# Attention: the reciprocals of the heads' sums as one power of minus one on GpSimd, in place of two reciprocals on VectorE

## The chip, the core and the metric

The kernel runs on one core of one Trainium2 chip. The metric is the device time of one execution in microseconds (us); the figure compared is the median over runs. The engines go by short names in the profile: PE is TensorE, DVE is VectorE, ACT is ScalarE, POOL is GpSimd, and SP is the engine whose queue issues nearly all of this kernel's DMAs. Each engine runs its own instruction stream in order, and semaphores tie the streams together.

## What is computed

The reference is one layer of a hybrid network on an input of 4 x 1024 tokens with 256 channels: attention with 16 heads of 16 channels, a feed-forward layer with ternary weights, a memory layer with a scan over time, and the feed-forward layer again, each behind a layer norm and with a residual. The change lies in the attention, which is cut to this:

```python
def _L0_attn_a_ref(x, ln_gamma, ln_beta, w_qkv, b_qkv, w_out, b_out):
    h = (x - mu) * rsqrt(var + 1e-05) * ln_gamma + ln_beta
    qkv = (h @ w_qkv + b_qkv).reshape(B, T, 3, NUM_HEADS, HEAD_DIM)
    scores = einsum('bhqd,bhkd->bhqk', q, k) / sqrt(HEAD_DIM)
    attn = softmax(scores, axis=-1)
    out = einsum('bhqk,bhkd->bhqd', attn, v)
    return x + out.reshape(B, T, C) @ w_out + b_out
```

## The kernel before

The kernel has three stages on a time axis: `project` (queries, keys and values, to about 105 us), `attend` (to about 795 us) and `mix_and_remember` (the rest). The change is in `attend`.

`attend` works through NG = 16 groups of four heads; four groups make one batch. Each group has two halves of 512 queries (qc = 0, 1), and each half has eight blocks of 128 keys (kt). For each block PE makes four score matrices of 128 keys x 512 queries (`score`, L758), ACT takes their exponential into `prob` (L663), and PE multiplies `prob` by the values (`weigh`, L770) into `ps_o`. The values tile `v_ones` has 16 columns of values and 16 of ones for each head, so `ps_o` holds the unnormalised output and, beside it, the sum of the exponentials. At the end of each half ACT copies `ps_o` to `o_sb` (`take_o`, L653) and SP stores it in DRAM as `oT` (`store`, L577).

The softmax needs each query's maximum before its scores are made. PE therefore computes the scores a second time, one half-group to one group ahead, for the maxima only (`score_for_max`, L747), into two buffers of `ps_m`. DVE reduces them (`maxima`, L684, 16 reductions of 128 x 1024 for each half). PE may not write a buffer of `ps_m` before DVE has reduced what it holds, and PE issues this work in between the scores and the weighing of the current half (`scores_ahead`). After the 16 reductions DVE makes five small steps: L687 takes the maximum of two interleaved parts of the tile `maxes`, which lies in SBUF, so both of its inputs are in SBUF; L689 and L691 negate and split; L696 transposes. SP then writes the transposed rows to DRAM (`place_max`, L569) and, when they have landed, reads them back into two rows of the queries' stack (L573). PE's first score of the half waits for this (`m_in`).

The division by the sums is done later, by reciprocals. For the three early batches (groups 0 to 11) the sums are gathered in one DMA into the tile `sums`, 96 partitions x 512 (L612, issued at the start of group 13). DVE inverts them in place in two operations of 96 x 256 (`invert`, L706), one behind each half of `maxima` of group 14, which DVE runs while PE is still in group 13 and early in group 14. SP, in its turn for group 14, first places the maxima of the half, then waits for both halves of `inverted` (L588), stores the reciprocals in DRAM (L589), waits for that store, issues eight loads for the first two chunks of the next stage (`load_heads`, L508 and L510), and only then stores group 14's first output and places the maxima of group 15's first half. POOL multiplies the loaded heads by the loaded reciprocals (`divide_heads`, L516). All these DMAs go through SP's one queue.

POOL has little to do in `attend`: it copies the values of a group into `v_ones` when the slot is free (`place_v`, L622); behind the copy for group 15, its last, come two small products (L636, L637) and then the wait of `divide_heads` for chunk 0. In other stages POOL computes powers: `scalar(const, which, shape)` gives one column of the tile `scalars`, repeated over the shape without a copy, and `tensor_tensor(..., ALU.pow)` raises a tile to that power. L101 and L245 do this with -0.5 on tiles of 2 to 8 columns.

Of the kernel before, what the change touches and what calls it, by code (L numbers as in the profile page):

```python
# [11 lines left out]
ALU = mybir.AluOpType  # L12
# [6 lines left out]
B, T, C = 4, 1024, 256  # L19
TOK = B * T  # L20
H, HD = 16, 16
CH = C // P
CHUNK = 512
# [3 lines left out]
LN_EPS = 1e-5  # L27
RMS_EPS = 1e-6
# [54 lines left out]

SCALARS = (-0.5, LN_EPS, RMS_EPS, 1.0, 0.0)
S_MINUS_HALF, S_LN_EPS, S_RMS_EPS, S_ONE, S_ZERO = range(5)


def scalar(const, which, shape):  # L90
    col = const["scalars"][:, which:which + 1]
    for _ in shape[2:]:
        col = col.unsqueeze(len(col.shape))
    return col.to_broadcast(shape)
# [10 lines left out]
NG = B * H // GH  # L105
# [28 lines left out]
def load_stacks(sp, qk_parts, stacks, g, slot):  # L134

    for qk, stack, part in ((0, stacks["q"], Q_PART), (1, stacks["k"], K_PART)):
        src = qk_parts[qk, bass.ds(g * CG, CG)].rearrange("(hp par d) a t -> par d a hp t", par=2, d=HD)
        for par, base in enumerate(BASES):
            for i in range(PAIRS):
                sp.dma_start(stack[slot][base + i * HD:base + (i + 1) * HD], src[par][:, part[i]]).then_inc(stacks["loaded"][slot], 16)  # L140


def project(nc, cols, rows, const, w, qk_parts, stacks, v_all, x_all, heads, rows_1):
# [5 lines left out]
    with ExitStack() as ctx:  # L149
# [73 lines left out]
        def _(pool):  # L223
# [3 lines left out]
            for tile, value in ((ident[:], 0.0), (ones[:], 1.0), (ln_mul[:, 0:1], 1.0), (ln_mul[:, 1:2], 1.0 + LN_EPS),  # L227
                                (ln_add[:, 0:1], LN_EPS), (ln_add[:, 1:2], LN_EPS ** 2)):
                made.did(pool.memset(tile, value))
            for j, value in enumerate(SCALARS):  # L230
                made.did(pool.memset(const["scalars"][:, j:j + 1], value))
# [260 lines left out]
def sums_of(oT, batches, per_head):  # L492

    rows = slice(batches.start * NG // B * P, batches.stop * NG // B * P)
    return oT[rows].rearrange("(h r) (j t) -> r h j t", r=2 * HD, j=per_head)[HD]


def inverses_of(inverse, batches, per_head):
    return inverse[batches.start * H:batches.stop * H].rearrange("h (j t) -> h j t", j=per_head)


def load_heads(sp, oT, inverse, heads, n):
    b, half = divmod(n, T // CHUNK)
    at = slice(half * CHUNK, (half + 1) * CHUNK)
    for c in range(CH):
        rows = (NG // B * b + 2 * c) * P
        src = oT[rows:rows + 2 * P, at].rearrange("(h two d) t -> two h d t", two=2, d=HD)[0]
        sp.dma_start(heads["o"][n % 2][:, c], src).then_inc(heads["loaded"][n % 2], 16)  # L508
        sums = inverse[H * b + H // CH * c:H * b + H // CH * (c + 1), at]
        sp.dma_start(heads["inverse"][n % 2][:, c], sums.unsqueeze(1).to_broadcast([H // CH, HD, CHUNK])).then_inc(heads["loaded"][n % 2], 16)  # L510
# [8 lines left out]
def attend(nc, rows, const, x_all, qk_parts, stacks, v_all, oT, inverse, heads, rows_1):  # L519
# [4 lines left out]
    with ExitStack() as ctx:  # L524
        def sb(name, shape, dt=F32):
            return ctx.enter_context(nc.sbuf_tensor(name, shape, dt))

        def sem(name):
            return ctx.enter_context(nc.semaphore("p2_" + name))
# [29 lines left out]
        sums, per_head = sb("sums", [2 * H * (B - 1), CHUNK]), 2  # L559
        sums_in, inverted, inverse_out = sem("sums_loaded"), sem("inverted"), sem("inverses_stored")  # L560
# [3 lines left out]
        @block.sync  # L564
        def _(sp):
            def place_max(g, slot, qc):
                half = QC * g + qc
                sp.wait_ge(m_turned, half + 1)
                sp.dma_start(neg_rows[qc].rearrange("(a b) (c i) -> c (a b) i", a=2, c=4), negT[qc][:]).then_inc(m_stored[qc], 16)  # L569
                sp.wait_ge(m_stored[qc], 16 * g + 16)  # L570
                rows_of = neg_rows[qc].rearrange("(a hp par t) q -> par a hp (t q)", a=2, hp=HP, par=2)
                for par, base in enumerate(BASES):
                    sp.dma_start(q_st[slot][base + MROW:base + ROWS, :, qc * CHUNK:(qc + 1) * CHUNK], rows_of[par]).then_inc(m_in[qc], 16)  # L573

            def store(g, qc):
                sp.wait_ge(o_taken, QC * g + qc + 1)
                sp.dma_start(oT[bass.ds(g * P, P), qc * CHUNK:(qc + 1) * CHUNK], o_sb[qc][:]).then_inc(o_out[qc], 16)  # L577

            def group(g, u, load_ahead=True, first=False, last=False, inverses=False):
                if load_ahead:  # L580
                    if not first:
                        sp.wait_ge(exp_done, EXPS * g + S_RING)
                    load_stacks(sp, qk_parts, stacks, g + 2, (u + 2) % SLOTS)
                if not first:
                    store(g - 1, 1)
                place_max(g, u, 1)
                if inverses:
                    sp.wait_ge(inverted, 2)  # L588
                    sp.dma_start(inverses_of(inverse, early, per_head), sums[:]).then_inc(inverse_out, 16)  # L589
                    sp.wait_ge(inverse_out, 16)  # L590
                    load_heads(sp, oT, inverse, heads, 0)
                    load_heads(sp, oT, inverse, heads, 1)
                if not last:
                    store(g, 0)
                    place_max(g + 1, (u + 1) % SLOTS, 0)
                else:
                    sp.wait_ge(out_ready, 2)
                    load_heads(sp, oT, inverse, heads, 2)
                    store(g, 0)
                    store(g, 1)  # L600

            place_max(0, 0, 0)
            for g in range(3):
                group(g, g, first=g == 0)
            for it in range(1, 4):
                for u in range(3):
                    group(3 * it + u, u)
            for g in range(12, NG):
                if g == NG - 3:
                    sp.wait_ge(o_out[0], 16 * g)  # L610
                    sp.wait_ge(o_out[1], 16 * (g - 1))
                    sp.dma_start(sums[:], sums_of(oT, early, per_head)).then_inc(sums_in, 16)  # L612
                group(g, g % 3, load_ahead=g + 2 < NG, last=g == NG - 1, inverses=g == NG - 2)
            for s in o_out:
                sp.wait_ge(s, 16 * NG)

        @block.gpsimd
        def _(pool):
            def place_v(g, slot, first=False):
                if not first:  # L620
                    pool.wait_ge(pv_done, UNITS * (g - 2) + 2)
                pool.tensor_copy(v_st[slot][:, :, :, 0:HD],  # L622
                                 v_all[:, bass.ds(g, 1)].rearrange("p g k (h d) -> p (g k) h d", d=HD)).then_inc(v_set, 1)

            for i in range(SLOTS):
                pool.memset(v_st[i][:, :, :, HD:], 1.0).then_inc(ones_set, 1)
                place_v(i, i, first=True)
            for n in range(NCH):
                at = x_all[:, TPC * n:TPC * n + TPC]
                pool.tensor_tensor(at, at, rows[:, ROW_BOUT:ROW_BOUT + 1].to_broadcast([P, TPC, C]), ALU.add).then_inc(bias_added, 1)  # L630
            for it in range(1, 5):
                for u in range(3):
                    place_v(3 * it + u, u)
            place_v(NG - 1, 0)
            norm_g = rows[:, ROW_NORMG:ROW_NORMG + 1]
            pool.tensor_tensor(const["w_gate"][:], const["w_gate"][:], norm_g.to_broadcast([P, CH, C]), ALU.mult).then_inc(bias_added, 1)  # L636
            pool.tensor_tensor(rows[:, ROW_GB:ROW_GB + 1], rows[:, ROW_GB:ROW_GB + 1], norm_g, ALU.mult).then_inc(bias_added, 1)  # L637
            divide_heads(pool, heads, 0)
            divide_heads(pool, heads, 1)
            pool.wait_ge(var_ready, 1)  # L640
            inverse_deviation(pool, Steps(pool, dev_steps), rows_1["mv"][:, 0, 0, :, 1], const, rows_1["tmp"][:, 0, 0], rows_1["rstd"][:, 0, 0], rstd_ready)
            divide_heads(pool, heads, 2)
            pool.wait_ge(bias_added, NCH + 2)
            pool.wait_ge(heads["divided"], 2)
# [32 lines left out]
        def _(dve):  # L677
# [22 lines left out]
            for g in range(2):  # L700
                maxima(g + 1, 0)
                maxima(g + 1, 1)
            def invert(k):
                dve.wait_ge(sums_in, 16)
                at = slice(k * CHUNK // 2, (k + 1) * CHUNK // 2)
                dve.reciprocal(sums[:, at], sums[:, at]).then_inc(inverted, 1)  # L706

            for it in range(1, 5):
                for u in range(3):
                    for qc in range(QC):  # L710
                        maxima(3 * it + u, qc)
                        if 3 * it + u == NG - 2:
                            invert(qc)
            maxima(NG - 1, 0)
            maxima(NG - 1, 1)

# [1525 lines left out]
```

## Time and profile before

| | us |
|---|---|
| median of 2 runs (lowest, highest) | 1155.38 (1152.81, 1157.96) |
| the profiled execution | 1156.36 |
| its span | 1154.3 |
| granted clock of PE, mean of the profiled execution | 0.962 of full speed |
| PE busy | 1064.9 (92%) |
| DVE busy | 1002.0 (87%) |
| ACT busy | 808.4 (70%) |
| POOL busy | 244.3 (21%) |

The profiled execution is 1.0 us above the median, and 2.1 us of it lie outside its span. The busy shares are averages over three stages with different limits. The groups of instructions show what carries `attend`: 1024 exponentials of ACT (555.8 us), 512 reductions of DVE (606.7 us), and the three kinds of matmul of PE at L747, L758 and L770 (219.4, 260.5 and 327.9 us). POOL's copies at L622 have 530.1 us of idle time ahead of them.

### The profile page before, as it was taken

The page shows a single profiled execution, that of the slowest core. Times are in us where ns is not written, and L with a number is a line of the kernel's source. Part 1 is how long each engine was busy: PE and PEld are TensorE (multiplying, and loading weights), DVE is VectorE, ACT ScalarE, POOL GpSimd, SP SyncE. Part 2 cuts the span into 40 slices and gives each one's busy share as a digit, 9 for nine tenths or more (in the row PEclk, how much of TensorE's full clock was granted, in tenths as well). Part 3 has the DMA queues.
Part 4 walks back from the last instruction along what each step waited for, and adds up shares of the span by engine and source line. Part 5 has one row for each costly group of instructions (what it writes and reads, how often), then busy time and mean ns, then how long its engine had stood idle before and what let it go on. Part 6 is the DMA issues. An engine that isn't in the chain of part 4 may idle for free. (4 is left out here: it accounts for less than half of the span.)

```text
span 1154.3 us, 22163 instructions
## 1 busy us (share of the span) xinstructions
PE 1064.9 (92%) x8566; PEld 582.3 (50%) x8566; DVE 1002.0 (87%) x1469; ACT 808.4 (70%) x1654; POOL 244.3 (21%) x345
## 2 busy tenths in 40 slices
PE   5997799999999999999999998997899998799995
PEld 4885233333333333333333333334667766688984
DVE  7776999999999999999999999943499998569887
ACT  4452288888888888888888887873568687343443
POOL 6423300000000000000000000102254333665643
PEclk9898599999999999999999999998899998899997
DMA  8595304414422440442244040211134325634321
GB/s 271 152 316 192 56 13 75 67 25 63 67 48 41 75 65 24 65 67 48 41 75 67 26 68 20 84 53 38 63 111 141 116 79 162 195 85 134 102 74 55
DMA packets 87332, 101.55 MB, mean 88 GB/s; under 512 B 21884, under 2 KB 57212, under 8 KB 87228
## 3 DMA queue, kind: packets, MB, share of 16 engines
q1 hardware_dynamic: 86396, 98.56, 35.8%
q8 instruction: 67, 1.10, 0.4%
q10 hardware_dynamic: 832, 1.58, 0.4%
q14 instruction: 37, 0.30, 0.1%
HBM read 55.09 MB, written 43.88 MB: 86 GB/s over the span
## 5 line engine op out<-in xcount | busy, mean ns | idle before, releaser
L663 ACT ACTIVATE prob<-ps_s 128x512 f32<-128x512 f32 x1024 | 555.8, 597 | 124.5 <-PE ps_s L758 107.6
L684 DVE TENSOR_REDUCE maxes<-ps_m 128x2 f32<-128x1024 f32 x512 | 606.7, 1217 | 18.1 <-PE ps_m L747 14.7
L770 PE MATMUL ps_o<-prob,v_ones 128*32 128x256 f32 x4096 | 327.9, 392 | 7.7 <-issue 7.3
L758 PE MATMUL ps_s<-q_stack,k_stack 64*128 64x512 f32 x1024 | 260.5, 499 | 0.0
L747 PE MATMUL ps_m<-k_stack,q_stack 62*128 62x512 f32 x1024 | 219.4, 422 | 17.9 <-DVE maxes L684 14.2
L758 PEld LDWEIGHTS ps_s<-q_stack,k_stack 64*128 64x128 f32 x1024 | 99.0, 184 | 211.3 <-ACT prob L663 187.6
L770 PEld LDWEIGHTS ps_o<-prob,v_ones 128*32 128x32 f32 x4096 | 81.7, 108 | 192.1 <-issue 102.7
L622 POOL COPY v_ones<-v_all 128x512 f32<-128x512 f32 x16 | 9.8, 614 | 530.1 <-PE ps_o L770 530.1
L747 PEld LDWEIGHTS ps_m<-k_stack,q_stack 62*128 62x128 f32 x1024 | 101.1, 192 | 35.2 <-DVE maxes L684 27.8
L405 ACT ACTIVATE p_parts<-ps_qk,cols 128x512 fp32r<-128x512 f32 x32 | 22.0, 687 | 39.2 <-PE ps_qk L450 33.2
L1385 PE MATMUL p_p<-p_hT,w_p 128*128 128x512 f32 x96 | 44.4, 613 | 2.6 <-ACT p_hT L1150 2.6
L516 POOL TENSOR_TENSOR heads<-heads,inverse 128x1024 f32<-128x1024 f32 x8 | 18.9, 2363 | 94.0 <-DMA inverse<-inverse_sums 94.0
L324 DVE SCALAR_TENSOR_TENSOR p_parts<-ps_qk,cols,p_parts 128x512 fp32r<-128x512 f32 x32 | 23.7, 745 | 11.9 <-ACT p_parts L405 11.5
L1313 PE MATMUL p_a<-w_gate,p_hT 128*128 128x256 f32 x128 | 31.5, 400 | 0.0
L1385 PEld LDWEIGHTS p_p<-p_hT,w_p 128*128 128x128 f32 x96 | 18.6, 197 | 23.5 <-issue 20.1
L99 POOL TENSOR_TENSOR ln_tmp<-ln_mv,scalars 128x4 f32<-128x4 f32 x16 | 11.1, 692 | 83.7 <-DVE ln_mv L73 83.7
L1313 PE MATMUL p_a<-w_out,heads 128*128 128x256 f32 x112 | 28.1, 408 | 0.1
L1313 PEld LDWEIGHTS p_a<-w_gate,p_hT 128*128 128x128 f32 x128 | 24.7, 198 | 4.3 <-issue 0.2
L69 DVE BATCH_NORM_STATS2 p_stats<-x_all 128x6 f32<-128x256 f32 x60 | 21.0, 413 | 6.1 <-DMA x_all<-in_x_dram 5.9
L1313 PEld LDWEIGHTS p_a<-w_out,heads 128*128 128x128 f32 x112 | 22.9, 210 | 3.8 <-issue 0.3
L1070 ACT ACTIVATE p_pre_kv<-p_p 128x512 f32<-128x512 f32 x8 | 4.8, 597 | 27.7 <-PE p_p L1385 27.7
L69 DVE BATCH_NORM_STATS2 ln_stats<-x_all 128x6 f32<-128x256 f32 x64 | 22.5, 414 | 0.6
(301 smaller groups left out, 1534.7 us busy)
## 6 DMA issues: line engine op xcount, KB each, us to landing
qk_parts<-p_parts SPq DMA_DIRECT2D x32, 512.0 KB, 7.4
q_stack<-qk_parts SPq DMA_DIRECT2D x96, 128.0 KB, 4.7
k_stack<-qk_parts SPq DMA_DIRECT2D x96, 128.0 KB, 7.7
oT<-o_sb SPq DMA_DIRECT2D x32, 256.0 KB, 4.1
x_all<-in_x_dram SPq DMA_DIRECT2D x8, 512.0 KB, 9.9
heads<-oT SPq DMA_DIRECT2D x16, 256.0 KB
inverse<-inverse_sums SPq DMA_DIRECT2D x16, 256.0 KB
out_dram<-x_all SPq DMA_DIRECT2D x7, 512.0 KB, 3.7
```

What stands on the lines that cost most here:

```text
L69: steps.did(dve.bn_stats(stats[:, i, :], src[:, i, :]))
L99: steps.did(pool.tensor_tensor(tmp, var, scalar(const, S_LN_EPS, tmp.shape), ALU.add))
L324: dve.scalar_tensor_tensor(out=r32(parts[:, n % 2, j, 1]), in0=ps_qk[:, j], scalar=cols[:, COL_BQK + j:COL_BQK + j + 1], in1=parts[:, n % ...
L405: act.activation(r32(parts[:, n % 2, j, 0]), ps_qk[:, j], ACT.Identity, bias=cols[:, COL_BQK + j:COL_BQK + j + 1]).then_inc(hi_ready, 1)
L516: pool.tensor_tensor(o[:], o[:], heads["inverse"][n % 2][:], ALU.mult).then_inc(heads["divided"], 1)
L663: act.activation(prob[at % P_RING][:, h], ps_s[:, (GH * at + h) % S_RING], ACT.Exp, scale=HD ** -0.5).then_inc(exp_done, 1)
L684: dve.tensor_reduce(maxes[:, i // 2, i % 2], ps_m[:, i % M_PAIRS], AX.X, ALU.max).then_inc(m_taken, 1)
L747: ins = pe.matmul(ps_m[:, i // 2 % M_PAIRS, i % 2], r32(q_st[slot][base:base + MROW, hp, q0:q0 + P]), r32(k_st[slot][base:base + MROW, hp, ...
L758: pe.matmul(ps_s[:, (GH * (UNITS * slot + KT * qc + kt) + h) % S_RING], r32(k_st[slot][rows, pair, kt * P:(kt + 1) * P]), r32(q_st[slot][r ...
L770: ins = pe.matmul(ps_o[32 * h:32 * h + 32, queries], v_st[slot][:, kt, h], prob[(UNITS * slot + KT * qc + kt) % P_RING][:, h, queries], st ...
L1313: ins = pe.matmul(ps_a[:, i // 2, i % 2], src[:, c, i * P:(i + 1) * P], weights[:, c], start=c == 0, stop=c == CH - 1)
L1385: ins = pe.matmul(ps_p[:, j], w_p[:, c, j * P:(j + 1) * P], hT[n % 2][:, c], start=c == 0, stop=c == CH - 1)
```

## The change

The list of constants gets a sixth entry, -1.0. `scalar` takes as many partitions as the shape asks for. The two reciprocals on DVE go. On POOL, behind the copy of values for group 15 and ahead of the two small products, comes a wait for the sums and one `tensor_tensor` with `ALU.pow` over the whole tile of 96 x 512, in place. SP waits for one step of `inverted` instead of two.

```diff
-SCALARS = (-0.5, LN_EPS, RMS_EPS, 1.0, 0.0)
-S_MINUS_HALF, S_LN_EPS, S_RMS_EPS, S_ONE, S_ZERO = range(5)
+SCALARS = (-0.5, LN_EPS, RMS_EPS, 1.0, 0.0, -1.0)
+S_MINUS_HALF, S_LN_EPS, S_RMS_EPS, S_ONE, S_ZERO, S_MINUS_ONE = range(6)
@@ scalar
-    col = const["scalars"][:, which:which + 1]
+    col = const["scalars"][0:shape[0], which:which + 1]
@@ attend, block.sync
                 if inverses:
-                    sp.wait_ge(inverted, 2)
+                    sp.wait_ge(inverted, 1)
@@ attend, block.gpsimd
             place_v(NG - 1, 0)
+            pool.wait_ge(sums_in, 16)
+            pool.tensor_tensor(sums[:], sums[:], scalar(const, S_MINUS_ONE, [2 * H * (B - 1), CHUNK]), ALU.pow).then_inc(inverted, 1)
@@ attend, block.vector
-            def invert(k):
-                dve.wait_ge(sums_in, 16)
-                at = slice(k * CHUNK // 2, (k + 1) * CHUNK // 2)
-                dve.reciprocal(sums[:, at], sums[:, at]).then_inc(inverted, 1)
-
             for it in range(1, 5):
                 for u in range(3):
                     for qc in range(QC):
                         maxima(3 * it + u, qc)
-                        if 3 * it + u == NG - 2:
-                            invert(qc)
```

## Rows read from the trace of the kernel before

**Rows 1.** The page's head: the span, and each engine's busy us and share.
```profile
span 1154.3 us, 22163 instructions
PE 1064.9 (92%) x8566; PEld 582.3 (50%) x8566; DVE 1002.0 (87%) x1469; ACT 808.4 (70%) x1654; POOL 244.3 (21%) x345
```
**Rows 2.** Windows (start:end, length, each engine's busy us, PE clock, DMA): half-groups without and with a reciprocal.
```profile
664.40:684.60 20.20, 19.97 (x194) 7.45 (x192) 19.64 (x21) 17.75 (x35) 2.40 (x3) 1.00 0.58 80
706.40:729.00 22.60, 20.94 (x188) 7.52 (x190) 20.88 (x22) 17.08 (x33) 0.00 (x0) 0.92 0.22 68
```
**Rows 3.** Waits, 664 to 750 us: PE for DVE's reductions (us in total, times, longest).
```profile
PE ps_m L747 <- DVE maxes L684: 3.2, 3, 1.4
```
**Rows 4.** Timeline of DVE (start, us, engine, line): L687 of one half; the two reciprocals.
```profile
672.62 0.19 DVE L687 TENSOR_TENSOR maxm<-maxes 128x16 f32<-128x16 f32 x1
...
693.60 1.71 DVE L706 RECIPROCAL sums<-sums 96x256 f32<-96x256 f32 x1
...
715.42 1.71 DVE L706 RECIPROCAL sums<-sums 96x256 f32<-96x256 f32 x1
```
**Rows 5.** Timeline of ACT: the copies that end halves, and group 15's first exponentials.
```profile
664.34 0.60 ACT L653 ACTIVATE o_sb<-ps_o 128x512 f32<-128x512 f32 x1
684.55 0.60 ACT L653 ACTIVATE o_sb<-ps_o 128x512 f32<-128x512 f32 x1
706.37 0.60 ACT L653 ACTIVATE o_sb<-ps_o 128x512 f32<-128x512 f32 x1
729.64 0.60 ACT L653 ACTIVATE o_sb<-ps_o 128x512 f32<-128x512 f32 x1
...
748.24 2.26 ACT L663 ACTIVATE prob<-ps_s 128x512 f32<-128x512 f32 x4 [0.22 <-PE ps_s L758]
```
**Rows 6.** All instructions of lines 245 and 101, powers on POOL (ns min/median/max).
```profile
L245 POOL TENSOR_TENSOR p_rstd<-p_var_eps,scalars x8: 1642/1703/1962, 7.4 to 67.6; 128x8 f32<-128x8 f32 x8
...
L101 POOL TENSOR_TENSOR ln_rstd<-ln_tmp,scalars x16: 1006/1009/1392, 773.9 to 950.9; 128x4 f32<-128x4 f32 x16
...
L101 POOL TENSOR_TENSOR p_rstd_last<-p_tmp_last,scalars x2: 696/696/697, 1140.3 to 1141.4; 128x2 f32<-128x2 f32 x2
```
**Rows 7.** Timelines of POOL and DVE: L687 started during POOL's sums and products, twice.
```profile
108.23 18.50 POOL L630 TENSOR_TENSOR x_all<-x_all,rows 128x1024 f32<-128x1024 f32 x8
...
124.41 2.37 DVE L687 TENSOR_TENSOR maxm<-maxes 128x16 f32<-128x16 f32 x1
...
736.20 2.37 POOL L516 TENSOR_TENSOR heads<-heads,inverse 128x1024 f32<-128x1024 f32 x1 [3.31 <-DMA inverse<-inverse_sums]
...
737.91 0.72 DVE L687 TENSOR_TENSOR maxm<-maxes 128x16 f32<-128x16 f32 x1
```
**Rows 8.** Timelines of POOL and DVE: a two-input DVE operation during a power of 8 columns.
```profile
10.49 1.68 POOL L245 TENSOR_TENSOR p_rstd<-p_var_eps,scalars 128x8 f32<-128x8 f32 x1
...
11.31 1.01 DVE L302 SCALAR_TENSOR_TENSOR p_wq_lo<-v_all,cols,p_wq_hi 128x768 fp32r<-128x768 f32 x1
...
12.25 1.05 POOL L247 TENSOR_TENSOR p_gain<-p_rstd,scalars 128x4 f32<-128x4 f32 x1
```
**Rows 9.** Timelines of SP and POOL: the sums, the reciprocals' store, group 15's maxima.
```profile
656.61 0.61 SPq L612 DMA_DIRECT2D sums<-oT  x1
...
664.25 0.62 POOL L622 COPY v_ones<-v_all 128x512 f32<-128x512 f32 x1 [39.79 <-PE ps_o L770]
...
718.75 0.39 SPq L589 DMA_DIRECT2D inverse_sums<-sums  x1
...
739.31 0.55 SPq L569 DMA_DIRECT2D neg_rows<-neg_maxT  x1
741.31 1.29 SPq L573 DMA_DIRECT2D q_stack<-neg_rows  x2
```
**Rows 10.** Windows as in Rows 2: PE behind the second reciprocal, and early in attention.
```profile
720.00:722.00 2.00, 2.00 (x14) 0.70 (x12) 1.60 (x2) 1.02 (x2) 0.00 (x0) 0.50 0.17 55
...
138.00:139.00 1.00, 1.00 (x11) 0.20 (x8) 1.00 (x2) 0.92 (x2) 0.00 (x0) 0.50 1.11 143
139.00:140.00 1.00, 1.00 (x12) 0.30 (x4) 0.86 (x1) 0.12 (x1) 0.00 (x0) 0.91 1.05 135
```

## The prediction, made before the changed kernel ran

> **What bounds the kernel now.** I read the page first: DVE is busy for 87% of the span and PE for 92%, POOL for 21% [rows 1]. Work that leaves DVE for POOL looks free by these shares, but they are averages, so I went to the windows of single half-groups around the change. A half without a reciprocal lasts 20.20 us, of which DVE is busy 19.64 and PE 19.97 [rows 2]. The two are locked together through the buffers of `ps_m`, and whatever delays DVE delays everything. The copies that end the halves show it: 20.21 us between the first two, 21.82 with the first reciprocal, 23.27 with the second [rows 5]. The waits name the cause, PE on DVE's reductions, once 1.4 us long behind each reciprocal [rows 3]. In the half with the second reciprocal PE's granted clock also falls, to 0.92 on average [rows 2] and to 0.50, its lower level of 1.2 GHz, from 720 to 722 us [rows 10]; PE had stood idle for the reduction just before.
>
> **What is removed.** Two reciprocals of 1.71 us [rows 4]. The first lengthened its half by 21.82 - 20.20 = 1.62 us. The second lengthened its own by 23.27 - 20.20 = 3.07 us, of which 1.45 is the slow clock. Together 4.7 us of the path. I take all of it, if no other wait takes their place.
>
> **What is added, by itself.** One power over 512 columns. The trace has powers of 2, 4 and 8 columns; their shortest durations are 696, 1006 and 1642 ns [rows 6]. The steps are (1006 - 696) / 2 = 155 and (1642 - 1006) / 4 = 159 ns a column, so the cost is 378 + 157 x columns, a straight line. Partitions lie side by side, so 96 instead of 128 save nothing that I count on. For 512 columns: 0.378 + 512 x 0.157 = 80.8 us, with 79.7 and 81.8 by the two slopes. From below, POOL's sum over 1024 columns takes 18.50 / 8 = 2.31 us [rows 7], so 1.2 us for 512, if the long tile ran at the rate of a plain operation. I take 80.8, because it comes from the same operation on the same engine and three sizes agree; the far end stays as a rival.
>
> It starts when POOL has copied the last values, at 664.25 + 0.62 = 664.87 us; the sums were asked for at 656.61 [rows 9], 8 us earlier, and are there. It ends at 664.9 + 80.8 = 745.7.
>
> **Where it lies: beside DVE.** POOL is idle at this time, and the power would be hidden if it touched nothing of DVE's. It does. L687 normally takes 0.19 us [rows 4]. Begun at 124.41, while POOL's sums ran until 108.23 + 18.50 = 126.73, it took 2.37 us and ended at 126.78. Begun at 737.91, while a product of POOL's ran until 738.57, it took 0.72 and ended at 738.63 [rows 7]. Both times it ended 0.05 us behind POOL: it did not slow down, it stood still until POOL's instruction was over. A power stands in the same place for far longer. L687 is due at 672.62, 7.8 us into the power. If it is held to the end, it ends at 745.7 + 0.05 instead of 672.81: 72.9 us later. L689, L691, the transpose and all later reductions are queued behind it on DVE; PE fills the two buffers of `ps_m` and stops within two steps; ACT runs out of scores. Nothing covers this.
>
> Against it stands one observation. A DVE operation with two SBUF inputs, L302, began at 11.31, inside a power of 8 columns that ran from 10.49 to 12.17, and took 1.01 us, ending at 12.32; it wasn't held. Right after it the order was turned round: POOL's L247, begun at 12.25, needed 1.05 us [rows 8] and waited for the next DVE operation. So a short power lets DVE in after at most 0.8 us, before its end. My reading is that POOL keeps DVE out while its inputs are still being read; 8 columns are read at the start, and the columns of a 512-column power are read as they are used, to within a few of the end. If the read-ahead is 8 columns, DVE is let in 8 x 0.157 = 1.3 us sooner. If instead the power reads in pieces with gaps, DVE gets in almost at once. The trace has no long power, so both ends stay: 72.9 and about 0. I take 72.9, since the two L687 cases are the same DVE instruction as here and the counter-example is 64 times shorter than the new operation.
>
> The Trainium skill says the same more sharply: "SBUF — State Buffer", section "Who interferes with whom", has GpSimd and a VectorE operation with two SBUF inputs exclude each other for the whole instruction, and whichever issues second blocks fully. The L687 rows agree with it; the 8-column power doesn't for its whole length. By this rule the sum is the one I take; by the counter-example it is that of the first rival.
>
> **The smaller terms.** POOL's L636 and L637 now follow the power and meet the DVE steps behind L687; where they alternate, L689 and L691 wait for them. Between 0 and 2 us; I take 1.0. PE has stood still for 70 us and starts at the lower clock: from 138 to 139 us it works with full busy time at 0.50, and is back at 0.91 in the next microsecond [rows 10]. The second reciprocal's episode cost 1.45 us. Between 0 and 4; I take 1.7. On SP the wait for the power is over long before its turn comes, since PE, ACT and DVE all stand still meanwhile: nothing. The extra constant is one more tiny fill at the start: nothing.
>
> **The sum**, against the profiled execution of 1156.4: 1156.4 + 72.9 + 1.0 + 1.7 - 4.7 = 1227.3. Against the median of the runs, which is 1.0 lower, it would be 1226.3. Nothing in the later stages can take this back, as they start only when attention ends. I give 1227.
>
> **Rival A: DVE is let in, and SP's queue becomes the bound.** The power still ends at 745.7, but DVE goes on. Without the reciprocals group 15's first exponentials are due at 748.24 - 4.7 = 743.5 [rows 5]. SP sits in its wait for `inverted` with the head loads, group 14's first store and group 15's maxima queued behind it. Before, the store of the reciprocals began at 718.75 [rows 9] and the last of the head loads had landed at 736.20, where POOL's product begins [rows 7]: 17.5 us. Now that is 745.7 + 17.5 = 763.2, and the maxima travel in the same queue behind them. After it come the read-back's two issues, 1.3 us [rows 9], and some 2 us of landing: 766.5. The first exponentials are 18.3 us later than before; with 1.7 for the clock the time is 1156.4 + 20.0 = 1176. If the small transfers pass the large ones, the maxima are issued after 7.5 us of head-load issues at 753.2, and with the 2.0 us from L569 to L573 [rows 9], 1.3 and 2 they land at 758.5: 1168. For it: rows 8. Against it: rows 7. It decides from the point where DVE's small steps get in between POOL's reads.
>
> **Rival B, on the other side: a long power is cheap.** If the 157 ns a column belong to short tiles and 512 columns run near the 2.3 ns a column of POOL's sums, the power takes about 1.6 us, ends before DVE's L687 is due at 672.62, and hides entirely: 1156.4 - 4.7 = 1151.7. It decides below 7.8 us with DVE held, or below about 50 us with DVE let in. Against it: three sizes on one line, no sign of a lower slope. In a sentence by itself: the Trainium skill, "GPSIMD Engine Reference", section "Elementwise — side-by-side cycle accounting", has about 2.6 cycles an element for `tensor_tensor`, which as an estimate is 1.1 us for 512 columns and would give this rival's time; rows 6 contradict it for the power.
>
> **How the numbers follow.** Forecast, DVE held to the power's end: 0.62, with its own range of 1215 to 1240 (the slope, 1.3 of read-ahead, 0 to 2, 0 to 4, and the 5 us by which runs of before differ). Rival A: 0.26, from 1164 to 1186. Rival B: 0.08, 1148 to 1156. The remaining 0.04 is a power dearer or cheaper by more than a tenth. From 1170 to 1240 lie nearly all of the forecast and most of rival A, about 8 in 10. A measurement of this kernel tells a change of about 2% from none, which is 1132 to 1178.5. Rival B and the part of rival A below 1178.5 lie inside: 0.08 + 0.13, so same 0.21. Faster than 1132 has no mechanism: 0.01. Slower 0.78.
>
> **What would show it.** Right: one POOL power of about 80 us from 665 us; one L687 of about 73 us in DVE's timeline, against 0.19; all 31 others as before; PE, ACT and SP empty from about 675 to 746; halves of 20.2 us before and behind. Rival A: L687 at 0.19 throughout, an empty stretch of some 20 us on PE from 743 us, and SP's store of the reciprocals at about 746. Rival B: a POOL power of a few us. I am wrong if the power's duration is off the straight line, or if POOL gives way to DVE within the instruction.

## The result, and the profile after

| | before, us | after, us |
|---|---|---|
| median | 1155.38 | 1177.81 |
| lowest and highest | 1152.81 and 1157.96 | 1176.92 and 1178.70 |
| profiled execution | 1156.36 | 1178.70 |
| its span | 1154.3 | 1176.8 |

The changed kernel is slower: its median is 22.4 us higher, and the ratio on record is 1.0178, with a 95% interval of 1.0141 to 1.0214. Each kernel has two runs here. The ratios in this text are the recorded ones; they differ from the ratios of the medians shown (here 1.0194) by up to 0.0016. The time lies inside the range that was given, but the forecast of 1227 was wrong by 49 us, and so was its mechanism. What happened is rival A, which had 1176 for the profiled execution, measured at 1178.7.

In the changed kernel the power is L636. L686 is the reduction (L684 before), L689 the maximum of two inputs in SBUF (L687 before), L753 the scores (L758), L742 the scores for the maxima (L747), L665 the exponentials (L663), L655 the copy that ends a half (L653), and L638 and L639 are POOL's two small products (L636 and L637).

First the timelines of POOL and DVE (start, duration, engine, line). They answer to [rows 4, 7] and to the last copy of values in [rows 9].

```profile
665.16 0.62 POOL L622 COPY v_ones<-v_all 128x512 f32<-128x512 f32 x1 [39.80 <-PE ps_o L765]
665.74 81.94 POOL L636 TENSOR_TENSOR sums<-sums,scalars 96x512 f32<-96x512 f32 x1
...
673.53 0.19 DVE L689 TENSOR_TENSOR maxm<-maxes 128x16 f32<-128x16 f32 x1
...
693.75 0.19 DVE L689 TENSOR_TENSOR maxm<-maxes 128x16 f32<-128x16 f32 x1
...
713.96 0.19 DVE L689 TENSOR_TENSOR maxm<-maxes 128x16 f32<-128x16 f32 x1
...
734.18 0.19 DVE L689 TENSOR_TENSOR maxm<-maxes 128x16 f32<-128x16 f32 x1
```

The power is there, in the place forecast and 1.1 us longer than forecast (80.8). Four times DVE's two-input maximum begins inside it, and four times it takes 0.19 us. The hold of 73 us doesn't exist.

The ends of the halves on ACT answer to [rows 5].

```profile
665.26 0.60 ACT L655 ACTIVATE o_sb<-ps_o 128x512 f32<-128x512 f32 x1
685.47 0.60 ACT L655 ACTIVATE o_sb<-ps_o 128x512 f32<-128x512 f32 x1
705.69 0.60 ACT L655 ACTIVATE o_sb<-ps_o 128x512 f32<-128x512 f32 x1
725.91 0.61 ACT L655 ACTIVATE o_sb<-ps_o 128x512 f32<-128x512 f32 x1
768.60 1.08 ACT L665 ACTIVATE prob<-ps_s 128x512 f32<-128x512 f32 x2 [24.84 <-PE ps_s L753]
772.17 0.60 ACT L655 ACTIVATE o_sb<-ps_o 128x512 f32<-128x512 f32 x1 [0.38 <-PE ps_o L765]
```

The halves from 685.47 last 20.22 and 20.22 us; before they lasted 21.82 and 23.27. So 4.65 us are gained, as the first step said. The next half lasts 46.26 us. Before it lasted 20.75, from 729.64 [rows 5] to this copy:

```profile
750.39 0.60 ACT L653 ACTIVATE o_sb<-ps_o 128x512 f32<-128x512 f32 x1
```

That half alone costs 25.5 us. The queue of SP and the waits (us in total, times, longest) tell why; before, the store of the reciprocals began at 718.75 and the maxima's write at 739.31 [rows 9].

```profile
716.81 1.22 SPq L573 DMA_DIRECT2D q_stack<-neg_rows  x2
747.70 0.34 SPq L589 DMA_DIRECT2D inverse_sums<-sums  x1
749.81 0.65 SPq L508 DMA_DIRECT2D heads<-oT  x1
...
754.22 0.72 SPq L510 DMA_DIRECT2D inverse<-inverse_sums  x1
754.98 0.62 SPq L577 DMA_DIRECT2D oT<-o_sb  x1
755.65 0.82 SPq L569 DMA_DIRECT2D neg_rows<-neg_maxT  x1
764.91 1.28 SPq L573 DMA_DIRECT2D q_stack<-neg_rows  x2
```
```profile
PE ps_s L753 <- DMA q_stack<-neg_rows: 24.3, 1, 24.3
```

SP issues nothing from 718 to 747.7, though DVE had transposed group 15's maxima at 735.0. It waits for the power, then issues eight loads of 256 KB (four of heads, four of reciprocals, which I call the head loads), and only then writes the maxima. From that write to the read-back 9.3 us pass, against 2.0 in [rows 9]; ahead of it in the same queue are these 2 MB, and the experiments below exchange the two. PE stands still for 24.3 us and goes on at 767.71.

Last, the windows (start:end, length, busy us of PE, PEld, DVE, ACT, POOL, PE clock, DMA) behind the stall, which answer to [rows 10].

```profile
769.00:771.00 2.00, 2.00 (x12) 0.56 (x9) 1.20 (x1) 0.98 (x3) 0.00 (x0) 0.50 0.00 0
771.00:773.00 2.00, 2.00 (x14) 0.70 (x12) 1.22 (x1) 1.46 (x4) 0.00 (x0) 0.56 0.00 0
773.00:775.00 2.00, 2.00 (x24) 0.79 (x24) 1.86 (x2) 1.89 (x4) 0.00 (x0) 1.00 0.33 131
```

PE is busy all the time but at the clock's lower level, 1.2 GHz, until about 772.8, with 12 to 14 matmuls in 2 us instead of 24. The half is 46.26 - 20.22 = 26.04 us longer than an undisturbed one: 24.26 of standing still, and the remaining 1.8, which I put down to the slow clock.

### The profile page after: what moved, and what is told of

Same layout as the page of the kernel before. It is cut to its first block and busy times, and to the rows that moved or that the text cites. A ratio compares the mean times of both kernels' runs of the same rounds, so it can differ in the third digit from the quotient of the medians.

```text
span 1176.8 us, 22163 instructions
## 1 busy us (share of the span) xinstructions
PE 1067.0 (91%) x8566; PEld 583.5 (50%) x8566; DVE 998.6 (85%) x1467; ACT 808.7 (69%) x1654; POOL 325.7 (28%) x347
## 5 line engine op out<-in xcount | busy, mean ns | idle before, releaser
L665 ACT ACTIVATE prob<-ps_s 128x512 f32<-128x512 f32 x1024 | 555.9, 597 | 145.9 <-PE ps_s L753 128.8
L686 DVE TENSOR_REDUCE maxes<-ps_m 128x2 f32<-128x1024 f32 x512 | 606.7, 1219 | 44.1 <-PE ps_m L742 40.8
L753 PE MATMUL ps_s<-q_stack,k_stack 64*128 64x512 f32 x1024 | 261.2, 501 | 24.3 <-DMA q_stack<-neg_rows 24.3
L742 PE MATMUL ps_m<-k_stack,q_stack 62*128 62x512 f32 x1024 | 219.6, 422 | 14.7 <-DVE maxes L686 11.0
L753 PEld LDWEIGHTS ps_s<-q_stack,k_stack 64*128 64x128 f32 x1024 | 99.1, 184 | 236.3 <-ACT prob L665 189.1
L742 PEld LDWEIGHTS ps_m<-k_stack,q_stack 62*128 62x128 f32 x1024 | 101.4, 193 | 31.6 <-DVE maxes L686 24.7
L636 POOL TENSOR_TENSOR sums<-sums,scalars 96x512 f32<-96x512 f32 x1 | 81.9, 81935 | 0.0
```

Source lines behind the costliest of these rows:

```text
L636: pool.tensor_tensor(sums[:], sums[:], scalar(const, S_MINUS_ONE, [2 * H * (B - 1), CHUNK]), ALU.pow).then_inc(inverted, 1)
L665: act.activation(prob[at % P_RING][:, h], ps_s[:, (GH * at + h) % S_RING], ACT.Exp, scale=HD ** -0.5).then_inc(exp_done, 1)
L686: dve.tensor_reduce(maxes[:, i // 2, i % 2], ps_m[:, i % M_PAIRS], AX.X, ALU.max).then_inc(m_taken, 1)
L742: ins = pe.matmul(ps_m[:, i // 2 % M_PAIRS, i % 2], r32(q_st[slot][base:base + MROW, hp, q0:q0 + P]), r32(k_st[slot][base:base + MROW, hp, ...
L753: pe.matmul(ps_s[:, (GH * (UNITS * slot + KT * qc + kt) + h) % S_RING], r32(k_st[slot][rows, pair, kt * P:(kt + 1) * P]), r32(q_st[slot][r ...
```

## The experiments

Medians are compared with runs of the kernel before on the same chip, which gave 1158.5, 1158.4 and 1159.8 in the three sets. Theories on record go by the letters that they had there.

**Without any reciprocals.** The sums are stored as they are.

```diff
-            pool.wait_ge(sums_in, 16)
-            pool.tensor_tensor(sums[:], sums[:], scalar(const, S_MINUS_ONE, ...), ALU.pow).then_inc(inverted, 1)
@@ block.sync
-                    sp.wait_ge(inverted, 1)
+                    sp.wait_ge(sums_in, 16)
```

> The changed kernel with the power left out as well: the early sums are stored as they are, so the heads of three batches are multiplied by the sums instead of divided by them, and SP waits for the sums only. Theory S (the loss is SP's wait for the power and the loads queued ahead of group 15's maxima; the power disturbs nothing else): the stall of 24.3 us on PE is gone and so are both reciprocals, so 1155.4 - 4.7 = 1150.7, ratio 0.996. Theory H (part of the loss is that POOL holds up DVE during the power): the same here. A theory that the reciprocals cost only their 1.71 us each and not the slow clock behind the second: 1155.4 - 3.4 = 1152.0.

The heads of the three early batches are then multiplied by the sums instead of divided by them. Measured: 1153.59 against 1158.48, ratio 0.9967 (0.9950 to 0.9984), so by the ratio 3.8 us less where 4.7 were expected. The stall is gone. The halves on ACT:

```profile
684.28 0.60 ACT L653 ACTIVATE o_sb<-ps_o 128x512 f32<-128x512 f32 x1
704.50 0.60 ACT L653 ACTIVATE o_sb<-ps_o 128x512 f32<-128x512 f32 x1
724.72 0.60 ACT L653 ACTIVATE o_sb<-ps_o 128x512 f32<-128x512 f32 x1
747.12 0.60 ACT L653 ACTIVATE o_sb<-ps_o 128x512 f32<-128x512 f32 x1
```

The two halves at the reciprocals last 20.22 us each, so the full 4.65 is there. The next one takes 22.40, 2.2 too many. The timelines of POOL and DVE show what moved:

```profile
733.17 2.37 POOL L516 TENSOR_TENSOR heads<-heads,inverse 128x1024 f32<-128x1024 f32 x1 [2.84 <-DMA inverse<-inverse_sums]
...
732.99 0.19 DVE L687 TENSOR_TENSOR maxm<-maxes 128x16 f32<-128x16 f32 x1
733.22 2.36 DVE L689 TENSOR_SCALAR neg_max<-maxm 128x16 fp32r<-128x16 f32 x1
735.61 0.17 DVE L691 SCALAR_TENSOR_TENSOR neg_max<-maxm,neg_max 128x16 f32<-128x16 f32 x1
```

POOL's second product of heads now falls on DVE's L689, which is held for its whole length. Before, the same product had met L687 only with its last 0.7 us [rows 7]. So 4.65 us is the worth of the reciprocals in their own place, and where the products land decides how much of it remains.

**Maxima before the wait.** In `group`, SP's block of wait, store and head loads moves behind `store(g, 0)` and `place_max(g + 1, ...)`.

```diff
-                if inverses:
-                    sp.wait_ge(inverted, 1)
-                    ...
                 if not last:
                     store(g, 0)
                     place_max(g + 1, (u + 1) % SLOTS, 0)
+                    if inverses:
+                        sp.wait_ge(inverted, 1)
+                        ...
```

> The changed kernel, only that SP stores group 14's first output and places group 15's maxima before it waits for the power, stores the reciprocals and loads the heads. Theory S: no stall at the start of group 15; the power ends at 747.7, the first heads land 11 us later, their product ends at about 761.1, and PE wants it 10.4 us after the start of group 15 at 743.5, at 754; a stall of 7 us there, and 1.5 for the clock: 1150.7 + 8.5 = 1159. Theory H (the power slows DVE or PE apart from SP's order): more than 1165, most of the loss stays.

Measured: 1163.62, ratio 1.0036 (1.0014 to 1.0057), 4.2 us above the kernel before by the ratio, where 3.6 were expected. So of the 1.8% by which the changed kernel is slower, 1.4 are gone by an order of issue alone. The power took the same 81.94 us beside the same work. What is left is one wait of PE, for the divided heads:

```profile
762.07 1.19 PE L796 MATMUL ps_m<-w_out,heads 128*128 128x256 f32 x2 [7.97 <-POOL heads L516]
```

7.0 was expected, 7.97 measured. The slow clock costs more than the 1.5 us expected: from 762 to 770 us PE's granted clock is 0.57 on average, and this last half lasts 34.05 us against 23.43 in the run with the wide power and the maxima first, 2.6 more than the wait. The halves up to there last 20.22 us each, although the power runs beside them. Theory S stands and H, that the power slows DVE or PE apart from SP's order, falls.

**Maxima before the heads.** SP keeps the wait and the store in their place, but issues the eight head loads behind group 15's maxima.

```diff
                     sp.wait_ge(inverse_out, 16)
-                    load_heads(sp, oT, inverse, heads, 0)
-                    load_heads(sp, oT, inverse, heads, 1)
                 if not last:
                     store(g, 0)
                     place_max(g + 1, (u + 1) % SLOTS, 0)
+                    if inverses:
+                        load_heads(sp, oT, inverse, heads, 0)
+                        load_heads(sp, oT, inverse, heads, 1)
```

> The changed kernel, only that SP, having waited for the power and stored the reciprocals, stores group 14's output and places group 15's maxima before it issues the eight head loads. It parts the stall of 24.3 us into the wait for the power and the transfers queued ahead of the maxima. Theory Q (transfers of one queue land in order, the maxima stood behind 2 MB of heads): maxima written at about 750.3, read back at 752.3, landed at 755, so a stall of 11.5 us instead of 24.3 and 1178 - 12.5 = 1165.5. If small transfers pass large ones, only the eight issues of 5 us are saved: a stall of about 19 us and 1173.

Measured: 1164.8, ratio 1.0047 (1.0028 to 1.0067). Between the profiled executions 15.2 us are gained (spans of 1176.8 and 1161.6), where 12.5 were expected. Timelines of SP and PE:

```profile
749.88 0.56 SPq L569 DMA_DIRECT2D neg_rows<-neg_maxT  x1
751.85 1.24 SPq L573 DMA_DIRECT2D q_stack<-neg_rows  x2
...
754.53 0.80 PE L754 MATMUL ps_s<-q_stack,k_stack 64*128 64x512 f32 x2 [11.40 <-DMA q_stack<-neg_rows]
```

With nothing ahead of them the maxima take 2.0 us again from write to read-back, and the stall is 11.4 instead of 24.3. So the stall of the changed kernel parts into 11.4 us that remain with the wait for the power, and 12.9 us of standing behind the heads. Of these, 5.5 lie between the reciprocals' store and the maxima's write, where SP issues the loads (7.95 us in the changed kernel, 2.5 here), and 7.3 from that write to the read-back. If small transfers passed large ones, only the first part would be there: theory Q.

**A long plain sum.** The kernel before, with POOL's eight sums at the start of attention as one, in the place of the power.

```diff
-            for n in range(NCH):
-                at = x_all[:, TPC * n:TPC * n + TPC]
-                pool.tensor_tensor(at, at, rows[...].to_broadcast([P, TPC, C]), ALU.add).then_inc(bias_added, 1)
@@ behind place_v(NG - 1, 0)
+            pool.tensor_tensor(x_all[:], x_all[:], rows[...].to_broadcast([P, NT, C]), ALU.add).then_inc(bias_added, NCH)
```

> The kernel before (both reciprocals on DVE), only that POOL's eight sums of 128 x 1024 at the start of attention are one sum of 128 x 8192 in the place where the change puts the power. It asks whether a long POOL instruction that isn't a power holds DVE's two-input maximum for its whole length. Theory W (held to the end): the sum runs from about 663 for 18.5 us, DVE's maximum begun at about 670.5 takes some 11 us and ends 0.05 us behind it; time 1155.4 - 2.2 (the hold at 124 us is gone) + 11 + 1.5 for the clock = 1165.7. Theory P (a POOL instruction lets DVE in between pieces, whatever it computes): the maximum takes at most 2.4 us, and the time is 1153 to 1156.

Measured: 1169.81 in one run, 11.3 above the kernel before of its set, where 10.3 were expected. Timelines of POOL and DVE:

```profile
663.49 17.62 POOL L632 TENSOR_TENSOR x_all<-x_all,rows 128x8192 f32<-128x8192 f32 x1
681.04 1.29 POOL L634 TENSOR_TENSOR w_gate<-w_gate,rows 128x512 f32<-128x512 f32 x1
...
671.28 9.86 DVE L685 TENSOR_TENSOR maxm<-maxes 128x16 f32<-128x16 f32 x1
681.18 1.17 DVE L687 TENSOR_SCALAR neg_max<-maxm 128x16 fp32r<-128x16 f32 x1
682.39 0.65 DVE L689 SCALAR_TENSOR_TENSOR neg_max<-maxm,neg_max 128x16 f32<-128x16 f32 x1
```

Here is the hold that I had forecast for the power. DVE's maximum (L685 in this kernel) takes 9.86 us and ends at 681.14, 0.03 behind POOL's sum. The next two steps are held by POOL's small products, for 1.5 us together, which I had put at 0 to 2. So a plain sum of 17.6 us does hold DVE to its end: theory W. The length alone doesn't explain why the power lets DVE in; the operation does.

**A long DVE operation inside the power.** The changed kernel, with the maximum of `x_all` with itself behind group 14's first half of maxima.

```diff
                         maxima(3 * it + u, qc)
+                        if 3 * it + u == NG - 2 and qc == 0:
+                            dve.wait_ge(bias_added, NCH)
+                            dve.tensor_tensor(x_all[:], x_all[:], x_all[:], ALU.max).then_inc(x_kept, 1)
```

> The changed kernel with one more DVE operation behind the first half of group 14's maxima, some 29 us into the power: the maximum of x_all with itself, 128 x 8192, two SBUF inputs, about 8.6 us, which leaves the values as they are. It asks why a power does not hold DVE. Theory P (the power reads its columns in pieces as it goes and lets go of the port in between): the DVE operation starts at once, and the power is held up in its turn once it wants its next piece, so it takes 82 + up to 8 us, 87 to 91. Theory A (the power reads all of its input within the first microseconds and computes from its own memory): the power stays at 81.9. In both the half with the DVE operation is 8 to 9 us longer; the end is 1178 under A, since SP waits for the power anyway and PE's start of group 15 moves from 743.5 to 752 while the maxima still land at 767; under P 5 to 9 us more, 1183 to 1187. A third theory, that the power would hold a long DVE operation to its end: DVE's operation takes about 50 us.

Measured: 1181.14, ratio 1.0194 (1.0156 to 1.0232), where the changed kernel itself has 1.0178. The power took 81.93 us, and DVE's operation began 29 us into it:

```profile
694.41 8.65 DVE L711 TENSOR_TENSOR x_all<-x_all 128x8192 f32<-128x8192 f32 x1
```

Neither held the other, as in theory A. A piece of the power's input that falls due at another moment was still possible.

**Four of them.** The same, four operations one behind the other.

```diff
+                            for k in range(4):
+                                dve.tensor_tensor(x_all[:], x_all[:], x_all[:], ALU.max).then_inc(x_kept, 1)
+                                dve.wait_ge(x_kept, k + 1)
```

> As the run with one long DVE operation inside the power, with four of them (8.65 us each, two SBUF inputs, values unchanged), one behind the other from some 29 to 64 us into the power. With one of them the power stayed at 81.93 us, which leaves two theories. Theory A (all of the power's input is read before): again 81.9. Theory L (it is read in large pieces, and the one operation happened to fall between two): a piece of any size below 220 columns falls due in these 35 us and waits for the operation then running, so the power takes 84 us or more. The half is 35 us longer in both; group 15 then starts at about 778, behind the maxima, so the time is about 1151.7 + 35 = 1186 to 1188 and SP's wait costs nothing.

Measured: 1191.0 in one run, 31 above the kernel before of its set; 1186 to 1188 had been 31 to 33 above 1155.4. Timelines of POOL and DVE:

```profile
662.24 81.94 POOL L636 TENSOR_TENSOR sums<-sums,scalars 96x512 f32<-96x512 f32 x1
...
691.02 34.83 DVE L712 TENSOR_TENSOR x_all<-x_all 128x8192 f32<-128x8192 f32 x4
```

DVE read two inputs in SBUF for 34.8 us nearly without a gap, and the power stayed at 81.94 us. During 35 of its 82 us it wanted nothing that DVE held. So it does not read column by column as it goes; that it has read everything before, theory A, fits but is not seen directly.

**A DVE operation with one input, inside the power.** It multiplies `x_all` by 1.0. That it also writes by a second way is an assumption of the expectation that no run shows.

```diff
+                            dve.tensor_scalar(x_all[:], x_all[:], 1.0, None, ALU.mult).then_inc(x_kept, 1)
```

> The changed kernel with one DVE operation behind the first half of group 14's maxima that has one SBUF input: x_all times 1.0, 128 x 8192, which leaves the values as they are. If it goes at two columns a cycle it takes about 4.3 us and also writes by its second way. It asks when the power writes. Theory E (all results at the end): DVE's operation takes 4.3 us and the power 81.9. Theory C (each column as it is ready): either DVE's operation is held until the power ends, 53 us, or the power is held for up to 4.3 us and takes up to 86. Time under E: 1178, since group 15's start stays behind the maxima at 767.

Measured: 1178.21 in one run. The power took 81.94 us, and DVE's operation half of the 8.65 us that two inputs took for the same columns:

```profile
694.28 4.38 DVE L711 TENSOR_SCALAR x_all<-x_all 128x8192 f32<-128x8192 f32 x1
```

That is theory E's outcome: neither held the other, though a plain product does hold an operation of this kind (L689 in the kernel without reciprocals). When the power writes its results is not shown by this.

**Short DVE operations at the power's start.** Eight of 128 x 64, released when POOL has copied the last values.

```diff
                 for i in range(M_MMS // 2):
+                    if half == QC * (NG - 3) + 1 and i == 10:
+                        dve.wait_ge(bias_added, NCH)
+                        dve.wait_ge(v_set, NG)
+                        for k in range(8):
+                            at = x_all[:, 4 * k, 0:64]
+                            dve.tensor_tensor(at, at, at, ALU.max).then_inc(x_kept, 1)
```

> The changed kernel with eight short DVE operations (x_all with itself, 128 x 64, two SBUF inputs, values unchanged, about 0.2 us each) that begin when POOL has copied the last values, which is when the power begins. It asks for how long the power holds DVE at its start. Theory A (the power reads its 512 columns and the constant in one go, at the 1.1 columns a ns at which POOL's plain sums stream, or the 2.15 ns a column of the long plain sum): one of the eight takes 0.5 to 1.3 us, the others 0.2. Theory P (it reads as it goes and shares): all eight take 0.2 us. Theory H (reads are spread and hold DVE): several are held. The power takes 81.9 or up to 0.3 more; the time is about that of the changed kernel, 1178.

Measured: 1181.61 in one run. Timelines of POOL and DVE:

```profile
665.20 81.93 POOL L636 TENSOR_TENSOR sums<-sums,scalars 96x512 f32<-96x512 f32 x1
...
665.35 1.27 DVE L690 TENSOR_TENSOR x_all<-x_all 128x64 f32<-128x64 f32 x1
...
666.54 0.77 DVE L690 TENSOR_TENSOR x_all<-x_all 128x64 f32<-128x64 f32 x1
...
667.37 0.21 DVE L690 TENSOR_TENSOR x_all<-x_all 128x64 f32<-128x64 f32 x1
```

The shortest of the eight took 0.21 us. The first ended at 666.62, the second at 667.31, and the others weren't held. Theory A had one held, and it was two, so the power keeps DVE out in two stretches, which are over 2.1 us after its start. (The 1.1 columns a ns that the expectation gives for plain sums is wrong: they take 2.15 to 2.3 ns a column, 17.62 us for 8192 and 2.31 for 1024.) After that DVE got in wherever it was tried: by the four L689 of the changed kernel, some 8, 28, 48 and 68 us into the power, and from 29 to 64 us by the four long operations. The last 13 us weren't tried. This is what the forecast had missed: this power holds DVE for 2.1 us, 4 ns for each of its 512 columns, and not for 160.

**The sums on all partitions, and the maxima first.** If a power costs by column, the 49152 sums are better laid on 128 x 384 than on 96 x 512: one load and one store for each batch, in SP's order of the run with the maxima before the wait.

```diff
-        early = slice(0, B - 1)
-        sums, per_head = sb("sums", [2 * H * (B - 1), CHUNK]), 2
+        early, per_head = [slice(b, b + 1) for b in range(B - 1)], P // H
+        sums = sb("sums", [P, B - 1, P])
@@ block.sync
-                    sp.dma_start(sums[:], sums_of(oT, early, per_head)).then_inc(sums_in, 16)
+                    for b in range(B - 1):
+                        sp.dma_start(sums[:, b], sums_of(oT, early[b], per_head)).then_inc(sums_in, 16)
@@ behind place_max(g + 1, ...)
+                        sp.wait_ge(inverted, 1)
+                        for b in range(B - 1):
+                            sp.dma_start(inverses_of(inverse, early[b], per_head), sums[:, b]).then_inc(inverse_out, 16)
```

> The reciprocals again by one power on POOL, but the sums lie on 128 partitions x 384 columns instead of 96 x 512 (three loads and three stores of 128 x 128 instead of one of each), and SP places group 15's maxima before it waits for the power, as in the run with the maxima before the wait. If the price is per column (160 ns from 81.94 us for 512), the power takes 0.4 + 384 x 0.159 = 61.5 us and ends at 727.5; SP comes to it at 738.5, the reciprocals are stored at about 741.5, the first heads have landed at 751 and are multiplied by 753.4, just before PE wants them at 754: no stall, 1150.7 to 1154 against a before of 1155.4 (ratio 0.995 to 0.999). If the price is per element whatever the partitions, the power stays at 81.9 us and the time at about 1163 as in the run with the maxima before the wait. It is meant to beat both kernels.

Measured: 1153.09 against 1158.36, ratio 0.9952 (0.9934 to 0.9969): by the ratio 5.6 us faster than the kernel before. It is the lowest ratio of all, though its interval overlaps that of the kernel without reciprocals. Timelines of POOL, and of ACT for the halves:

```profile
667.72 61.54 POOL L638 TENSOR_TENSOR sums<-sums,scalars 128x384 f32<-128x384 f32 x1
...
752.16 2.38 POOL L516 TENSOR_TENSOR heads<-heads,inverse 128x1024 f32<-128x1024 f32 x1 [20.95 <-DMA inverse<-inverse_sums]
...
687.48 0.60 ACT L657 ACTIVATE o_sb<-ps_o 128x512 f32<-128x512 f32 x1
707.70 0.60 ACT L657 ACTIVATE o_sb<-ps_o 128x512 f32<-128x512 f32 x1
727.91 0.60 ACT L657 ACTIVATE o_sb<-ps_o 128x512 f32<-128x512 f32 x1
748.11 0.60 ACT L657 ACTIVATE o_sb<-ps_o 128x512 f32<-128x512 f32 x1
```

All halves last 20.2 us. The power is 20.4 us shorter for the same number of elements, 61.54 / 81.94 = 0.751 for 384 / 512 = 0.75 of the columns, so from 96 to 128 partitions cost nothing and only columns count. POOL's products of heads fall on none of DVE's small steps.

**The wide power alone**, with SP's order as in the changed kernel; the edit is the one above without the move.

> The changed kernel, only that the sums lie on 128 partitions x 384 columns (three loads, three stores); SP's order is that of the changed kernel. By columns the power ends at 727.5 instead of 747.7, so SP's wait ends 20 us sooner; but its eight head loads are still ahead of group 15's maxima, which land at about 749 where PE wants them at 743.5: a stall of 5 us instead of 24.3, and 1 us for the clock: 1156 to 1158. If the price is per element, 1178 as the changed kernel.

Measured: 1159.44, ratio 1.0007 (0.9985 to 1.0030), 1.1 us above the kernel before where 0.6 to 2.6 were expected. PE waits for group 15's maxima, which are again behind the head loads (us in total, times, longest):

```profile
PE ps_s L755 <- DMA q_stack<-neg_rows: 4.2, 1, 4.2
```

Both halves of the remedy are needed: the shorter power alone takes the ratio from 1.0178 to 1.0007, the order of issue alone to 1.0036 (the maxima before the wait), and both together to 0.9952.

## Why the prediction was wrong, step by step

**What bounds the kernel** was right: the halves go by DVE and PE in lock-step, and both reciprocals came off the path in full, 4.65 us of 4.7.

**The power's price** was right and slightly low: 81.94 us instead of 80.8. From 512 and 384 columns the slope is (81.94 - 61.54) / 128 = 159 ns a column, the upper of the two slopes in [rows 6], and 0.34 us remain for the start. A line through 2, 4 and 8 columns held up to 512. That fewer partitions save nothing was assumed in a half-sentence and is now measured from 96 to 128; taken seriously it gives the remedy.

**Where it lies: beside DVE** is the step that failed: the hold put at 72.9 us measured nothing, since the maximum took 0.19 us all four times. It had two parts. "POOL keeps DVE out while its inputs are still being read" fits the runs, though none shows the reads themselves: the long plain sum held DVE to its end, and the power did so at its start. "The columns of a 512-column power are read as they are used" is false: all that was seen to hold DVE is over 2.1 us after the start, 5.7 us before L687 came, and for 35 us in the middle the power wanted nothing that DVE held. I had transferred the hold from plain operations, where it lasts as long as the instruction, to an operation some 70 times slower a column. The observation of [rows 8], a power of 8 columns that let DVE in at half its length, was the one row on this operation, and I set it aside for being short. It got 0.26 where it should have had more than half. The Trainium skill, "SBUF — State Buffer", section "Who interferes with whom" and the row on both engines in its summary of rules for kernel authors, has whichever of the two issues second blocked until the first has finished. The plain sum agrees with it (9.86 us), the power does not (DVE was held in 2.1 of 81.94 us).

**The smaller terms.** The 1.0 us for the products behind the power did not arise, since DVE's small steps came at another time; the long plain sum showed it at 1.5. The clock's 1.7 came out at 1.8, though PE had stood still for 24 us and not for 70. "On SP the wait for the power is over long before its turn comes", put at nothing, depended on the failed step. Once DVE goes on, this wait and the loads behind it are the loss: 24.3 us of stall on PE.

**Rival A, which came true,** had 1176 against 1178.7 for the profiled execution. Its terms: the power's end at 745.7, measured 747.7 (a start 0.9 later and 1.1 of price); 17.5 us from there to the landing of the heads, whose second product began at 763.96, 16.3 after; the maxima behind the heads in the queue, confirmed by exchanging them, 12.9 us; group 15's first exponentials at 766.5, measured 768.60. From the landing to the exponentials 4.6 us passed instead of 3.3. These terms missed by +2.0, -1.2 and +1.3 us and in part cancel, which is luck. Sum over the profiled executions: +0.9 before the change's place, -4.65 for the reciprocals, +25.5 for the long half, and +0.7 over the rest make the 22.5 us between the spans.

**Rival B** fell with the price. Its size for a power that hides entirely, 1151.7, or 0.9959 of 1156.4, is close to what the kernel with the hidden power shows, 0.9952.

## What to carry to other kernels

An idle engine is room for work only if the result is back before its reader wants it; here the work moved was 24 times dearer (81.94 us against 3.4), and the deadline stood in SP's queue, in a wait with the next half's maxima behind it. Put urgent issues ahead of a wait for something that is not urgent, and ahead of bulk loads in the same queue. When two rows disagree about a conflict, weigh first the row with the same operation as the new one, even if it is small, and ask what resource is held and for which part of the instruction.

## What the runs showed of the hardware that I had not expected

- A power on POOL costs 159 ns a column at 96 partitions as at 128 (61.54 us for 128 x 384, 81.94 for 96 x 512), and was seen to hold DVE's two-input operations only in the first 2.1 us of 82, in two stretches. A plain sum of 8192 columns costs 2.15 ns a column (17.62 us) and held DVE for all the time that they overlapped, 9.8 us.
- For 35 us in the middle of a power DVE ran operations with two inputs in SBUF without lengthening it (81.94 us with and without).
- A DVE operation with one input (L689 in the kernel without reciprocals, 2.36 us instead of 0.17) was held by POOL's product to its end, as one with two is.
